# One routed-expert transformer block: where the first expert's third weight piece is split into two halves

## The chip, the core and the metric

The kernel runs on one core of a Trainium2 chip. The number that counts is the device time in microseconds (us) of one execution. TensorE (PE) multiplies matrices, VectorE (DVE), ScalarE (ACT) and GpSimd (POOL) compute element by element, and SyncE (SP) issues most of the DMAs. Each engine runs its own instructions in order; they meet through semaphores only.

## The reference

The block takes x (4 batches of 1024 tokens, 256 wide) and does two steps, each added to x:

```python
x = x + tanh(g_xattn) * xattn(layernorm(x), ctx, ctx, mask)      # 77 keys per batch
x = x + tanh(g_ffn) * ffn(layernorm(x))
# ffn: every token goes to the one expert (of 8) with the largest router probability
logits = x @ router_w + router_b
for e in range(8):
    a, g = split(x @ w1[e]); y = silu(a) * g @ w2[e]     # w1[e] 256 x 2048, w2[e] 1024 x 256
    out = where(argmax == e, y, out)
out = out * max_prob
```

## The kernel before

**Attention loop.** The 1024 positions are cut into 8 groups of 128, each for all 4 batches. A software pipeline of 10 iterations (`for i in range(NG + 2)`) exists on each engine: in iteration i, PE makes the scores of group i and attends for group i - 2, ACT copies transposed x out of PSUM and takes the exponentials, DVE adds the mask, finds the maximum, adds the attention to x (L810) and takes the statistics of the second layernorm (L819, L825), POOL turns these into a reciprocal root and the router's logits (`norm2`, L423 to L432).

**Weights as two halves.** The expert matmuls run in a format that keeps part of a float32's bits. Every weight w is therefore held as w_hi (the rounded value) and w_lo = w - w_hi, and the products with w_hi and w_lo are added up. An expert has three pieces of 2048 columns (`PIECES` = 3): the two halves of w1 along the contraction (`DC` = 2), then w2. A piece is loaded by SP into `staging`, copied by ACT into `w_hi`, and POOL writes `w_lo` = `staging` - `w_hi`. For the first expert this is done in six chunks of 1024 columns (`N_CHUNK` = 6, chunks 4 and 5 are the third piece): `high0(c)` on ACT (L597) at the end of iteration c, `low0(c)` on POOL (L439) at the end of iteration c + 1. After every second chunk POOL raises `w_ready`. All other experts' pieces are split inside the expert loop (L723 on ACT, L511 on POOL).

**Building the lists.** When the last logits are there, each engine leaves the loop. DVE takes the argmax, sums the exponentials that ACT made (L659), writes the gate (L869), and turns counts and ranks into the position of each token in a list sorted by expert (L876 to L892). It then builds, in three rounds, one-hot tables in float16 (L908, L910, L913) that PE multiplies (L1133) into the list of indices; between the rounds PE runs matmuls whose result nobody reads (L1138). POOL writes two index ramps (iota, L460 and L462) for these tables before. It waits then for the first list (`lists_ready`) and gathers the rows of the first 128 sorted tokens with an indirect DMA (L467). ACT has nothing to do until it copies the tables of tile numbers out of PSUM (L663).

**Expert loop.** 35 tiles of 128 sorted tokens. For each, PE does the products with w1 (`up`, L1161), transposes, and those with w2 (`down`, L1179). The first tile's `up` waits for `w_ready`; in the loop, `down` of the tile before waits for `w_ready` of its own expert's third piece, an existing wait (`old * PIECES + PIECES`). SP's load of the second expert's third piece into `staging` waits for `w_ready` at 3, and that of the first piece for 1.

Of the kernel before, what the change touches and what calls it, by code (L numbers as in the profile page):

```python
# [27 lines left out]
def flamingo_block(nc, x, ctx_kv, mask, g_xattn, g_ffn, w1, b1, w2, b2, router_w, router_b, e_w1, e_w2, out):  # L28
    B, S, D = x.shape
    KEYS = ctx_kv.shape[1]  # L30
    E, _, F2 = e_w1.shape
    F = F2 // 2
    DC = D // P
# [13 lines left out]
    PIECES = 3  # L47
    PW = F2
# [26 lines left out]
    with ExitStack() as top:  # L75
# [5 lines left out]
        def sem(name):  # L81
            return top.enter_context(nc.semaphore(name))
# [214 lines left out]
        w_ready = sem("w_ready")  # L297
# [18 lines left out]
        W_CHUNK = PW // 2  # L316
# [2 lines left out]
        QUARTERS = 4  # L319
        QW = PW // QUARTERS  # L320
        N_CHUNK = PIECES * PW // W_CHUNK

        block = top.enter_context(nc.Block())

# [41 lines left out]
        def _(pool):  # L366
# [28 lines left out]
            def norm1(first_group, end_group):  # L395
                n = (end_group - first_group) * B
                at = slice(first_group, end_group)
                if first_group == 1:
                    pool.wait_ge(square_ready, 1)
                    link(nc.gpsimd.tensor_scalar(var_eps1[:, 1], x_square[:], 1.0 / D, EPS, ALU.mult, ALU.add))  # L400
                else:
                    pool.wait_ge(mv1_ready, end_group if end_group == 1 else end_group - 1)
                    link(nc.gpsimd.tensor_scalar(var_eps1[:, at], mv1[:, at, :, 1], EPS, None, ALU.add))
                nc.gpsimd.tensor_tensor(out=rstd1[:, at], in0=var_eps1[:, at],
                                        in1=minus_half[:, 0:n].rearrange("p (g b) -> p g b", b=B),
                                        op=ALU.pow).then_inc(rstd1_ready, end_group - first_group)

            def mask1(g):
                if g == 0:
                    pool.wait_ge(mask_loaded, 16)  # L410
                    pool.wait_ge(bias_ready, 1)
                if g >= 2:
                    pool.wait_ge(masked_ready, g - 1)
                nc.gpsimd.tensor_tensor(out=mask_c[:, g % 2], in0=bias_c[:].rearrange("p (b k) -> p b k", b=B),
                                        in1=mask_in[:, g:g + 1, :].to_broadcast([P, B, KEYS]),
                                        op=ALU.add).then_inc(mask_c_ready, 1)

            def norm2(g):
                r = g % 2
                pool.wait_ge(mv2_ready, g + 1)  # L420
                if g >= SHARED:
                    pool.wait_ge(half2_ready, g - SHARED + 1)
                link(nc.gpsimd.tensor_scalar(var_eps2[:, r], mv2[:, r, :, 1], EPS, None, ALU.add))  # L423
                link(nc.gpsimd.tensor_tensor(out=x_all[:, g, :, 1], in0=var_eps2[:, r], in1=minus_half[:, 0:B], op=ALU.pow))  # L424
                link(nc.gpsimd.tensor_tensor(out=logit_tmp[:], in0=x_all[:, g, :, KEPT:XROW],
                                             in1=x_all[:, g, :, 1:2].to_broadcast([P, B, E]), op=ALU.mult))
                if g == 0:
                    pool.wait_ge(router_b_loaded, 16)
                nc.gpsimd.tensor_tensor(out=logits[:, g * B:(g + 1) * B], in0=logit_tmp[:],
                                        in1=router_b_all[:].unsqueeze(1).to_broadcast([P, B, E]),  # L430
                                        op=ALU.add).then_inc(logits_ready, 1)
                nc.gpsimd.tensor_tensor(out=x_all[:, g, :, 0], in0=mv2[:, r, :, 0], in1=x_all[:, g, :, 1],  # L432
                                        op=ALU.mult).then_inc(rstd2_ready, 1)

            def low0(c):

                pool.wait_ge(w_hi_ready, c + 1)
                at = slice(c * W_CHUNK, (c + 1) * W_CHUNK)
                lo = nc.gpsimd.tensor_tensor(out=w_lo[:, at], in0=staging[:, at], in1=w_hi[:, at].bitcast(FP32),  # L439
                                             op=ALU.subtract)  # L440
                if c % 2:
                    lo.then_inc(w_ready, 1)
# [7 lines left out]
            for i in range(NG + 2):  # L450
                if i + 2 < NG:
                    mask1(i + 2)
                if 0 <= i - 2 < NG:
                    norm2(i - 2)
                if i < NG - EARLY:
                    norm1(EARLY + i, EARLY + i + 1)
                if 0 <= i - 1 < N_CHUNK:
                    low0(i - 1)
            pool.wait_ge(first_stored, 16 * FIRST)
            nc.gpsimd.iota(slot_iota[:], [[1, P], [0, B]], base=0, channel_multiplier=0,  # L460
                           allow_small_or_imprecise_dtypes=True)
            nc.gpsimd.iota(col_iota[:], [[1, COLS], [0, B]], base=0, channel_multiplier=0,  # L462
                           allow_small_or_imprecise_dtypes=True).then_inc(iotas_ready, 1)


            def gather_rows(t, index):
# [36 lines left out]
            def low_part(t):  # L503

                piece = pool.value_load(tile_piece[:, bass.ds(t, 1)], min_val=0, max_val=E * PIECES - 1)
                with pool.If(piece > 0):
                    src = pool.snap((piece % PIECES) * PW)
                    dst = pool.snap(((piece // PIECES) & 1) * EW + src)
                    pool.wait_ge(w_hi_ready, piece + (N_CHUNK - PIECES + 1))
                    for q in range(QUARTERS):  # L510
# [28 lines left out]
        def _(act):  # L539
# [25 lines left out]
            def copy_xt(g):  # L565
                act.wait_ge(xt1_psum, g + 1)
                if g >= 2:
                    act.wait_ge(scores_psum, g - 1)
                for k in range(DC):
                    last = nc.scalar.copy(x_t[:, g % 2, k], ps_xt[k][:])  # L570
                last.then_inc(xt1_ready, 1)
# [20 lines left out]
            def high0(c):  # L592

                if c % 2 == 0:
                    act.wait_ge(piece_loaded, 16 * (c // 2 + 1))
                at = slice(c * W_CHUNK, (c + 1) * W_CHUNK)
                nc.scalar.copy(w_hi[:, at], staging[:, at]).then_inc(w_hi_ready, 1)  # L597

            def copy_pt(g):
                act.wait_ge(pt_psum, g + 1)  # L600
                if g >= 2:
                    act.wait_ge(attn_psum, B * (g - 1))
                nc.scalar.copy(probs_t[:, g % 2], ps_p[0:KEYS, :]).then_inc(pt_ready, 1)

            def copy_logits(g):
                act.wait_ge(masked_ready, g + 1)
                scored = ps_s[g % 2][:, 0:B * KW].rearrange("p (b k) -> p b k", b=B)
                nc.scalar.copy(x_all[:, g, :, KEPT:XROW], scored[:, :, KEYS:KW]).then_inc(x_logits_ready, 1)

            def softmax(g):  # L610
                r = g % 2
                act.wait_ge(max_ready, g + 1)
                if g >= 2:
                    act.wait_ge(pt_psum, g - 1)
                    act.wait_ge(inv_ready, g - 1)
                for b in range(B):
                    last = nc.scalar.activation(probs[:, r, b], masked[:, r, b], ACT.Exp, bias=neg_max[:, r, b:b + 1],
                                                accum_out=prob_sum[:, r, b:b + 1])
                last.then_inc(probs_ready, 1)

            for i in range(NG + 1):
                if i + 1 < NG:
                    copy_xt(i + 1)
                if 0 <= i - 1 < NG:
                    copy_pt(i - 1)
                if i < NG:
                    copy_logits(i)
                    softmax(i)
                if i < N_CHUNK:
                    high0(i)  # L630


# [23 lines left out]
            for part, (first_group, end_group) in enumerate(PARTS):  # L656
                at = slice(first_group * B, end_group * B)
                act.wait_ge(centered, part + 1)
                nc.scalar.activation(work_e[:, at], work_b[:, at], ACT.Exp).then_inc(gate_exp, 1)  # L659


            act.wait_ge(tab_psum, 1)
# [325 lines left out]
        def _(pe):  # L988
# [153 lines left out]
            def transpose_x(t):  # L1142

                pe.wait_ge(xnorm_ready, t + 1)
                for k in range(DC):
                    last = nc.tensor.transpose(px[:, k * P:(k + 1) * P], x_norm[:, k * P:(k + 1) * P], ident[:])  # L1146
                last.then_inc(xt_psum, 1)
# [36 lines left out]

            pe.sem_inc(down_psum[1], 1)
            transpose_x(0)
            pe.wait_ge(w_ready, PIECES)
            pe.wait_ge(lists_ready, 2)
            up(0, 0, 0)
            up(0, 1, 0)  # L1190
# [56 lines left out]
```

## Time and profile before

| what | us |
|---|---|
| median of 3 runs (lowest, highest) | 437.21 (436.66, 441.84) |
| the profiled execution, its own time | 438.43 |
| its span, first to last instruction | 436.4 |
| PE busy in it | 401.4 (92%) |
| DVE, ACT, POOL busy | 194.4, 212.2, 239.7 |

The span is what the trace covers; the execution's own time is 2.03 us longer. In the span, the attention loop and what is prepared for it end at about 68 us, the lists are built up to 84.1 us, and the expert tiles follow from 89.9 us. "Busy" counts computing instructions alone; what decides is which engine the others wait for in each stage.

### The profile page before, as it was taken

What the parts mean: (1) busy time and instruction counts of PE and PEld (TensorE: products, weight loads), DVE (VectorE), ACT (ScalarE), POOL (GpSimd) and SP (SyncE); (2) the same over time, 40 slices, a digit from 0 to 9 for tenths busy, and PEclk for the clock granted to TensorE, in tenths of its full rate; (3) what the DMA queues carried; (4) which work ended last, traced back from release to release, by engine and by line L of the source; (5) the groups of instructions that cost most, each with busy time, mean ns of one, the idle gap of its engine ahead of it and who ended that gap; (6) DMA issues with size and microseconds to landing.
All of it is one profiled execution on the core that took longest, in us unless ns stands there. A gap on an engine that the chain in (4) does not pass through costs nothing.

```text
span 436.4 us, 9945 instructions
## 1 busy us (share of the span) xinstructions
PE 401.4 (92%) x2460; PEld 349.5 (80%) x2461; DVE 194.4 (45%) x464; ACT 212.2 (49%) x456; POOL 239.7 (55%) x315
## 2 busy tenths in 40 slices
PE   7988981679999999999999999999999999999990
PEld 7887860458888888888888888888888888888880
DVE  2888998714334343333434333333343343334330
ACT  2785752047536556645633364455534563433330
POOL 2588885115774887778842267648732785322221
PEclk9998997689999999999999999999999999999996
DMA  7952225634540333444331014403340010010010
GB/s 204 355 176 98 97 99 147 107 112 128 206 135 24 120 120 118 177 149 151 120 120 30 30 63 172 132 19 120 120 132 24 21 31 24 24 36 16 24 36 12
DMA packets 29850, 44.01 MB, mean 101 GB/s; under 512 B 8377, under 2 KB 25581, under 8 KB 27791
## 3 DMA queue, kind: packets, MB, share of 16 engines
q1 hardware_dynamic: 24095, 34.45, 24.5%
q0 software_dynamic: 3456, 9.11, 6.5%
q10 hardware_dynamic: 2288, 0.33, 0.5%
q8 instruction: 4, 0.07, 0.1%
q14 instruction: 7, 0.06, 0.0%
HBM read 35.44 MB, written 8.83 MB: 101 GB/s over the span
## 4 chain that ended last, share of the span: by engine, by line
PE 78%; DVE 8%; DMA 4%; SPq 3%; issue 3%; ACT 1%; POOL 1%; POOLq 0%; DVEq 0%; ACTq 0%
PE pa L1161 22%; PE pg L1161 22%; PE py L1179 22%; PE ph L1171 7%; SPq L333 3%; DMA staging<-in_L_ffn_w 2%; DVE x_all L810 2%; PE px L1146 2%; DVE bn L819 1%; PE ps_s L1083 1%; DVE masked L791 1%; DMA x_sorted<-residual_rows,idx_gather 1%; PE ps_xt L997 1%; DMA out<-out_tile,idx_now 1%; POOL x_all L424 0%
## 5 line engine op out<-in xcount | busy, mean ns | idle before, releaser
L511 POOL TENSOR_TENSOR w_lo<-staging,w_hi x84 | 105.9, 1290 | 6.5 <-ACT w_hi L723 3.9
L954 DVE TENSOR_TENSOR ht_lo<-ph,ht_hi 128x512 fp32r<-128x512 f32 x70 | 48.4, 692 | 133.9 <-ACT ht_hi L700 133.9
L700 ACT CAST ht_hi<-ph 128x512 fp32r<-128x512 f32 x70 | 41.1, 588 | 119.2 <-PE ph L1171 85.8
L1179 PE MATMUL py<-w_hi,ht_hi 128*128 x272 | 78.9, 290 | 0.0
L1179 PE MATMUL py<-w_hi,ht_lo 128*128 x272 | 76.1, 280 | 0.0
L1179 PE MATMUL py<-w_lo,ht_hi 128*128 x272 | 76.0, 279 | 0.0
L500 POOL DMA_INDIRECT out<-out_tile,idx_now x34 | 34.7, 1021 | 73.5 <-DVE out_tile L962 73.2
L1161 PE MATMUL pa<-w_hi,xt_hi 128*128 (+1 forms) x140 | 58.5, 418 | 0.8 <-ACT xt_hi L672 0.8
L467 POOL DMA_INDIRECT x_sorted<-residual_rows,idx_now x34 | 35.7, 1049 | 38.4 <-ACT residual L688 20.8
L1161 PE MATMUL pg<-w_hi,xt_hi 128*128 (+1 forms) x140 | 55.9, 399 | 0.0
L1161 PE MATMUL pa<-w_lo,xt_hi 128*128 (+1 forms) x140 | 55.9, 399 | 0.0
L1161 PE MATMUL pa<-w_hi,xt_lo 128*128 (+1 forms) x140 | 55.8, 399 | 0.0
L1161 PE MATMUL pg<-w_hi,xt_lo 128*128 (+1 forms) x140 | 55.8, 398 | 0.0
L1161 PE MATMUL pg<-w_lo,xt_hi 128*128 (+1 forms) x140 | 55.3, 395 | 0.0
L949 DVE TENSOR_TENSOR hidden<-pg,silu 128x512 f32<-128x512 f32 x70 | 48.1, 687 | 8.1 <-ACT silu L694 4.9
L1179 PEld LDWEIGHTS py<-w_lo,ht_hi 128*128 128x128 f32 x272 | 51.2, 188 | 0.0
L1179 PEld LDWEIGHTS py<-w_hi,ht_hi 128*128 128x128 f32 x272 | 51.2, 188 | 0.0
L1179 PEld LDWEIGHTS py<-w_hi,ht_lo 128*128 128x128 f32 x272 | 51.1, 188 | 0.0
L723 ACT CAST w_hi<-staging x21 | 40.2, 1912 | 9.7 <-PE py L1179 7.8
L694 ACT ACTIVATE silu<-pa 128x512 f32<-128x512 f32 x70 | 42.3, 605 | 3.5 <-PE pg L1161 3.5
L1171 PE MATMUL ph<-ident,hidden 128*128 128x128 f32 x280 | 41.9, 272 | 0.0
L942 DVE TENSOR_TENSOR xt_lo<-px,xt_hi 128x256 fp32r<-128x256 f32 x36 | 15.3, 424 | 59.0 <-ACT xt_hi L672 59.0
(194 smaller groups left out, 630.1 us busy)
## 6 DMA issues: line engine op xcount, KB each, us to landing
staging<-in_L_ffn_w SPq DMA_DIRECT2D x24, 1024.0 KB
residual_rows<-x_all SPq DMA_DIRECT2D x8, 516.0 KB, 3.8
x_all<-in_x SPq DMA_DIRECT2D x8, 512.0 KB, 10.0
x_sorted<-residual_rows,idx_now POOLq DMA_INDIRECT x34
out<-out_tile,idx_now POOLq DMA_INDIRECT x34, 2.5
w_in<-in_L_xattn_W SPq DMA_DIRECT2D x2, 256.0 KB, 4.7
ctx_in<-in_ctx SPq DMA_DIRECT2D x1, 308.0 KB
mask_in<-in_fside_1xSxS ACTq DMA_DIRECT2D x1, 308.0 KB, 11.6
```

The source lines that it names most:

```text
L467: pool.indirect_dma_start(x_sorted[:], None, rows, bass.IndirectOffsetOnAxis(ap=index, axis=0), bounds_check=last_row(t), oob_is_err=False ...
L500: pool.indirect_dma_start(out_rows, bass.IndirectOffsetOnAxis(ap=idx_now[:, 1:2], axis=0), tile_rows[:], None, bounds_check=limit, oob_is_ ...
L511: lo = nc.gpsimd.tensor_tensor(out=w_lo[:, bass.ds(dst + q * QW, QW)], in0=staging[:, bass.ds(src + q * QW, QW)], in1=w_hi[:, bass.ds(dst ...
L694: nc.scalar.activation(silu[:, j], pa[j][:], ACT.Silu).then_inc(silu_ready[j], 1)
L700: nc.scalar.copy(ht_hi[:, j], ph[j][:]).then_inc(hhi_ready[j], 1)
L723: nc.scalar.copy(w_hi[:, bass.ds(slot + src, PW)], staging[:, bass.ds(src, PW)]).then_inc(w_hi_ready, 1)
L942: nc.vector.tensor_tensor(out=xt_lo[:], in0=px[:, 0:D].rearrange("p (k n) -> p k n", k=DC), in1=xt_hi[:].bitcast(FP32), op=ALU.subtract).t ...
L949: nc.vector.tensor_tensor(out=hidden[:, j], in0=pg[j][:], in1=silu[:, j], op=ALU.mult).then_inc(hidden_ready[j], 1)
L954: nc.vector.tensor_tensor(out=ht_lo[:, j], in0=ph[j][:], in1=ht_hi[:, j].bitcast(FP32), op=ALU.subtract).then_inc(hlo_ready[j], 1)
L1161: last = mm(ps[:], xt[:, k], w[:, bass.ds(slot + (k * PW + col), HALF)], start=n == 0, stop=n == 3 * DC - 1)
L1171: last = nc.tensor.transpose(ph[j][:, c * P:(c + 1) * P], hidden[:, j, c * P:(c + 1) * P], ident[:])
L1179: last = mm(into[:, 0:D], ht[:, j, c * P:(c + 1) * P], w[:, bass.ds(slot + (DC * PW + (j * HC + c) * D), D)], start=j == 0 and n == 0, sto ...
```

## The change

Chunks 4 and 5, the two halves of the third piece, leave the loop on ACT and POOL. ACT does `high0(4)` and `high0(5)` after its last exponential, POOL does `low0(4)` and `low0(5)` after its second iota. PE's first `up` now waits for two pieces instead of three. Chunks 0 to 3 stay where they are; no instruction is added or dropped.

```diff
+        LOOP_CHUNK = DC * PW // W_CHUNK
...
                 if i < NG - EARLY:
                     norm1(EARLY + i, EARLY + i + 1)
-                if 0 <= i - 1 < N_CHUNK:
+                if 0 <= i - 1 < LOOP_CHUNK:
                     low0(i - 1)
             pool.wait_ge(first_stored, 16 * FIRST)
             nc.gpsimd.iota(slot_iota[:], [[1, P], [0, B]], base=0, channel_multiplier=0,
                            allow_small_or_imprecise_dtypes=True)
             nc.gpsimd.iota(col_iota[:], [[1, COLS], [0, B]], base=0, channel_multiplier=0,
                            allow_small_or_imprecise_dtypes=True).then_inc(iotas_ready, 1)
+            for c in range(LOOP_CHUNK, N_CHUNK):
+                low0(c)
...
-                if i < N_CHUNK:
+                if i < LOOP_CHUNK:
                     high0(i)
...
                 nc.scalar.activation(work_e[:, at], work_b[:, at], ACT.Exp).then_inc(gate_exp, 1)
+            for c in range(LOOP_CHUNK, N_CHUNK):
+                high0(c)
...
-            pe.wait_ge(w_ready, PIECES)
+            pe.wait_ge(w_ready, DC)
```

POOL's order before, from the end of iteration 6 to the first gather; L439 is `low0(5)`, and `low0(4)` stands seven rows above it:

```order
L439 TENSOR_TENSOR w_lo<-staging,w_hi 128x1024
L423 TENSOR_SCALAR var_eps<-mv 128x4
...
L432 TENSOR_TENSOR x_all<-mv,x_all 128x4
L460 IOTA slot_iota 128x512
L462 IOTA col_iota 128x220
L467 DMA x_sorted<-residual_rows,idx_gather 128x259 x3
```

POOL's order in the changed kernel, for the same place (its lines count one more from here on):

```order
L424 TENSOR_SCALAR var_eps<-mv 128x4
...
L433 TENSOR_TENSOR x_all<-mv,x_all 128x4
L461 IOTA slot_iota 128x512
L463 IOTA col_iota 128x220
L440 TENSOR_TENSOR w_lo<-staging,w_hi 128x1024 x2
L470 DMA x_sorted<-residual_rows,idx_gather 128x259 x3
```

Both subtractions now stand between the iotas and the gather, behind the last `norm2`.

ACT's order before, iteration 5 of the loop and, after the dots, the place behind the loop (L597 is `high0`, L659 the exponentials for the gate, L663 the tables):

```order
L617 ACTIVATE probs,prob_sum<-masked,neg_max 128x77 x4
L597 CAST w_hi<-staging 128x1024
L570 COPY x_t<-ps_xt 128x512 x2
...
L659 ACTIVATE work_e<-work_b 128x224
L659 ACTIVATE work_e<-work_b 128x32
L663 CAST tables<-ps_p 4x128
```

and in the changed kernel:

```order
L620 ACTIVATE probs,prob_sum<-masked,neg_max 128x77 x4
L573 COPY x_t<-ps_xt 128x512 x2
...
L662 ACTIVATE work_e<-work_b 128x224
L662 ACTIVATE work_e<-work_b 128x32
L600 CAST w_hi<-staging 128x1024 x2
L668 CAST tables<-ps_p 4x128
```

The two copies stand behind the gate's exponentials and ahead of the tables' copy.

## Rows read from the trace of the kernel before

**Rows 1.** The page, part 4: shares of the chain that ended last

```profile
PE 78%; DVE 8%; DMA 4%; SPq 3%; issue 3%; ACT 1%; POOL 1%; POOLq 0%; DVEq 0%; ACTq 0%
```

**Rows 2.** Timeline, ACT, loop: start us, us, instruction, [idle before <- releaser]

```profile
47.66 1.07 ACT L570 COPY x_t<-ps_xt 128x512 f32<-128x512 f32 x2 [1.48 <-PE ps_xt L997]
...
50.56 1.04 ACT L597 CAST w_hi<-staging 128x1024 fp32r<-128x1024 f32 x1
52.73 1.07 ACT L570 COPY x_t<-ps_xt 128x512 f32<-128x512 f32 x2 [1.12 <-PE ps_xt L997]
```

**Rows 3.** Timeline, POOL, loop, around chunks 4 and 5

```profile
54.78 2.36 POOL L439 TENSOR_TENSOR w_lo<-staging,w_hi 128x1024 fp32r<-128x1024 f32 x1
57.60 0.23 POOL L423 TENSOR_SCALAR var_eps<-mv 128x4 f32<-128x4 f32 x1 [0.46 <-DVE mv L825]
...
62.95 0.23 POOL L423 TENSOR_SCALAR var_eps<-mv 128x4 f32<-128x4 f32 x1 [0.87 <-DVE mv L825]
```

**Rows 4.** Timeline, DVE: L810 beside a POOL subtraction (43.74), and without one (62.96)

```profile
43.74 1.79 DVE L810 SCALAR_TENSOR_TENSOR x_all<-ps_o,prob_inv,x_all 128x264 f32<-128x264 f32 x4 [1.53 <-PE ps_o L1092]
...
62.96 1.79 DVE L810 SCALAR_TENSOR_TENSOR x_all<-ps_o,prob_inv,x_all 128x264 f32<-128x264 f32 x4
```

**Rows 5.** Timeline, ACT and POOL, list building: what bounds the idle stretches

```profile
86.45 0.26 ACT L663 CAST tables<-ps_p 4x128 int32<-4x128 f32 x1 [14.66 <-PE ps_p L1140]
...
72.35 0.59 POOL L462 IOTA col_iota<- 128x220 f16 x1
84.77 1.30 POOL L467 DMA_INDIRECT x_sorted<-residual_rows,idx_gather  x1 [11.83 <-DVE idx_scatter L923]
```

**Rows 6.** Timeline, DVE, list building: five of its instructions

```profile
73.07 0.24 DVE L869 TENSOR_SCALAR gate<-recip,tanh_g 128x32 f32<-128x32 f32 x1
...
73.23 0.68 DVE L876 TENSOR_TENSOR_SCAN cum<-restart,ps_xt 128x256 f32<-128x256 f16 x1
...
73.95 0.17 DVE L878 TENSOR_SCALAR counts_i<-cum 128x8 int32<-128x8 f32 x1
...
74.57 0.17 DVE L881 TENSOR_TENSOR_SCAN bounds<-restart,tiles_f 128x8 f32<-128x8 f16 x1
...
75.30 0.42 DVE L885 TENSOR_TENSOR work_a<-work_a,shift 128x256 f32<-128x256 f32 x1
```

**Rows 7.** The chain in order of time: start us, us, what

```profile
73.31 0.61 DVE cum L876
...
93.67 0.43 PE pa L1161
...
99.43 0.23 PE pa L1161
```

**Rows 8.** Timeline, DVE and POOL, three pairs of overlapping instructions

```profile
11.15 0.29 DVE L761 COPY bq_wide<-bq 128x256 f32<-128x256 f32 x1
11.16 0.37 POOL L403 TENSOR_SCALAR var_eps<-mv 128x4 f32<-128x4 f32 x1 [7.92 <-DVE mv L743]
...
70.26 0.39 DVE L862 TENSOR_TENSOR onehot<-expert_m,first 128x224 f16<-128x224 f32 x1
70.37 0.38 POOL L425 TENSOR_TENSOR logit_tmp<-x_all 128x32 f32<-128x32 f32 x1
...
69.25 1.04 POOL L424 TENSOR_TENSOR x_all<-var_eps,minus_half 128x4 f32<-128x4 f32 x1
69.41 0.39 DVE L858 SCALAR_TENSOR_TENSOR work_a<-work_b,expert_m 128x224 f32<-128x224 f32 x1
```

**Rows 9.** Timeline, POOL: the two stretched forms elsewhere

```profile
18.25 0.23 POOL L403 TENSOR_SCALAR var_eps<-mv 128x4 f32<-128x4 f32 x1 [0.36 <-DVE mv L743]
...
64.39 0.24 POOL L425 TENSOR_TENSOR logit_tmp<-x_all 128x32 f32<-128x32 f32 x1
```

**Rows 10.** Windows: stretch, us, PE busy, PEld, DVE, ACT, POOL, PEclk, DMA share, GB/s

```profile
75.00:78.00 3.00, 0.00 (x0) 0.00 (x0) 2.79 (x9) 0.00 (x0) 0.00 (x0) 0.50 0.98 42
...
91.00:94.40 3.40, 3.40 (x10) 2.66 (x9) 0.00 (x0) 0.07 (x1) 0.02 (x1) 0.51 0.22 49
```

## The prediction

> **What bounds the kernel now.** I read the shares of the chain of waits first: PE holds 78% of it and DVE 8% [rows 1]. Those shares are an average over stages, so I then read the chain in order of time around the two places that the change touches. In the attention loop it runs through DVE almost without a break. From 73.31 us, while the lists are built, it runs through DVE again and through PE's list matmuls, up to POOL's first gather at 84.77; in the expert tiles it runs through PE [rows 5, 7]. So the first place, which loses work, and the second, which gets it, are both stages where DVE sets the pace. The question is whether ACT's and POOL's work costs DVE anything in either.
>
> **What leaves the loop.** On ACT, two copies of 1.04 us. Behind the later one ACT sits idle for 1.12 us until PE has transposed the next group [rows 2]; the earlier one is followed by 1.48 us of such idling. Work that is followed by a longer wait for somebody else wasn't on the path, so the gain is 0. On POOL, two subtractions of 2.36 us. Behind the first POOL waits 0.46 us for DVE's statistics, behind the second 0.87 us [rows 3]: gain 0 too. Nor do these subtractions slow DVE in the loop: L810, which has one operand in SBUF and one in PSUM, takes 1.79 us for four both beside a subtraction and without one [rows 4]. A gain above 0 would need a wait that the rows don't show. Its upper bound is what POOL gives up, 2 x 2.36 = 4.7 us, and the rows with idle behind them place it at 0. I take 0.
>
> **What is added behind the loop, on ACT.** The two copies, 2.1 us, go into an idle stretch of 14.66 us that ends at 86.45 and so begins at 71.79 [rows 5]. They would run from 71.7 to 73.8. What covers them is ACT's wait for the tables, and 12 us of it are left. Cost 0. DVE's sum of exponentials isn't delayed, since the copies stand behind them.
>
> **On POOL.** The iotas end at 72.94, the gather follows at 84.77 after 11.83 us of idling [rows 5]. Two subtractions of 2.36 us fit: `low0(4)` from 72.9 to 75.25 (its w_hi half is there at 72.75), `low0(5)` at the earliest from 75.2 to 77.6. The gather queued behind them isn't reached by that time, so directly they cost 0. The wait for `w_ready` 3 moves from PE's first `up` at 89.9 to its first `down`, later still, and at 77.6 it is long met. SP's loads that wait for `w_ready` 1 and 2 are fed by chunks that don't move, and the load that needs 3 stands in SP's queue behind the wait for the second gather, which comes after 84.77. All 0.
>
> **The indirect cost: DVE beside POOL.** This is the term that decides. In the new place the subtractions read SBUF without pause for 4.7 us, and DVE runs its chain of small dependent steps beside them. Unlike L810, many of these have all operands in SBUF: L869 and L878 are tensor-by-scalar operations with source and result there, L881 and L885 read two SBUF tensors each [rows 6]. Two pairs of the trace show that such DVE instructions and POOL's exclude each other. POOL's L403 takes 0.37 us when it starts 0.01 us behind DVE's 256-column copy, and ends 0.09 us after that copy; elsewhere it takes 0.23. POOL's L425 takes 0.38 us beside DVE's two-input L862, and ends 0.10 us after it; elsewhere 0.24 [rows 8, 9]. In both POOL came second and was held by 0.14 us until DVE was done. A third pair speaks against the reverse: POOL's L424 was running for 0.16 us when DVE's two-input L858 started, and L858 took its usual 0.39 [rows 8]. But L424 handles four elements in 1.04 us, so it hardly reads, while a subtraction of 1024 columns reads all the time; for that no DVE instruction of the exposed kinds overlaps anywhere in this trace. So the bounds are:
> - none held: 0.
> - only two-input instructions held, subtractions as whole units: L881, due at 74.57, goes at 75.25 (+0.7). `low0(5)` gets in behind it and runs to about 77.8. L885, due at 75.30 + 0.7, goes at 77.8: 77.8 - 75.3 = +2.5.
> - tensor-by-scalar held as well, DVE served between the two subtractions: L869, due at 73.07, goes at 75.2 (+2.1). `low0(5)` gets in behind it, 75.4 to 77.8. L876 reads PSUM and one SBUF tensor and passes [rows 6]. L878, due at 73.95, goes at 77.8: +3.9.
> - POOL keeps its turn for both: L869 goes at 77.6, 77.6 - 73.07 = +4.5.
>
> I take +3.9: the first of the exclusion pairs is a copy, a one-input instruction like the tensor-by-scalar ones, and in both pairs the loser waited for the whole instruction. A hold on DVE here isn't absorbed, because the chain has no gap from 73.31 to the gather [rows 7]: PE's list matmuls, `lists_ready`, the gather and the first `up` all come 3.9 us later. The ends 0 and 4.5 make the range. A DVE instruction that starts first holds POOL instead, but POOL has 7 us in hand.
>
> The Trainium skill, "SBUF — State Buffer", section "Who interferes with whom", says just this of the shared port pair: a DVE instruction with two SBUF inputs, against POOL instructions that read SBUF, or in a two-port mode (copy, cast, tensor_scalar), shuts out POOL or is shut out by it for the whole instruction, whoever issues first. By that rule the term is the third bound, and it speaks against this change. The trace agrees for the two pairs in which DVE came first (0.14 us each) and doesn't for the pair in which POOL did.
>
> **TensorE's clock.** It stands at 0.50 (1.2 GHz) from 75 to 78 us, with PE idle, and at 0.51 from 91.0 to 94.4, with PE busy throughout [rows 10]. In that last stretch some 8 matmuls follow one another at 0.43 instead of 0.23 us [rows 7], 8 x 0.2 = 1.6 us lost against 2.4 GHz. If the first tile starts later, this stretch could move, vanish or repeat. No row says which; I enter 0 with ends of -1.6 and +1.6.
>
> **The sum.** 0 - 0 + 0 + 3.9 = +3.9 us on the span of 436.4, so 440.3. The profiled execution took 438.43, 1.2 us above the median; the median of 437.21 lies 0.8 us above the span. I forecast for the median: 437.2 + 3.9 = **441.1 us**.
>
> **Rivals.**
> 1. *Nothing is held* (the other side: no slower). POOL's long subtraction lets DVE read in between, as L424 did with L858. Everything moved lies under DVE's chain: 437.2. It decides as soon as a hold lasts a few hundredths of a microsecond instead of the whole 2.36. For it: the third pair. Against it: the two stretched POOL instructions. Chance 0.22.
> 2. *The loop gets shorter*, by a coupling that the rows don't show, say half of POOL's smaller slack turned around, or the clock's dip at 91 vanishes: -0.5 to -1.6, so 435.6 to 436.7. For it, nothing but that the loop loses 6.8 us of ACT and POOL work. Chance 0.06.
> 3. *Held, and the clock's dip lasts longer or comes twice*: +3.9 + 1.6, so 442.7, up to 443.3 with +4.5. PE's idle stretch ahead of its list matmuls would grow by the 3.9 us, at a clock that is at 0.50 in it already [rows 10]. Against it: the matmuls that nobody reads (L1138) stand between list and first tile as before. Chance 0.12.
> 4. *The forecast*, pair held, with its smaller form of +2.5 (439.7): chance 0.60.
>
> **Range and chances.** The likeliest time is 441.1. The range is 436.3 to 443.3: its upper end is that of rival 3, its lower end takes in half of rival 2. In between lie the forecast in its forms, the no-hold case and most of rival 3; for the noise of runs some of each falls outside, which leaves about 0.8. About 2% (8.7 us) is what a measurement of this kernel can tell from no change, its runs having spread over 5 us. None of the cases reaches it: within 2% 0.95, slower 0.04 for a second loss on top of the hold, faster 0.01.
>
> **What would show each step.** In the changed profile: both subtractions at about 72.9 and 75.4; the gate's L869 lasting some 2.3 us instead of 0.24, or starting late, and the count step L878 some 1.8 instead of 0.17; the sum over the DVE instructions between 73 and 84 larger by 3.9, their number unchanged. The gather at about 88.7 instead of 84.77. The loop ending at the same time as before. From the first `up` to the end the same length, within 1.5. I would be wrong if every small DVE step kept its 0.17 beside the subtractions (rival 1), if the loop ended earlier (rival 2), or if the hold were real but ended with each of POOL's reads, giving some tenths in all.

## The result, and the profile after

Over 22 executions each, the changed kernel's median is 441.16 us (lowest 440.00, highest 446.92), that of the kernel before 438.38 (436.57 to 444.39). The ratio is 1.0059, 95% interval 1.0036 to 1.0083: slower by some 2.6 us (1.6 to 3.6 us), well inside 2%. The lowest executions differ by 3.43 us. The forecast was 441.1 us, and +3.9 against before, which lies above that interval. (Executions of either kernel lie between 436 and 448 us, with a mean granted clock of TensorE between 0.971 and 0.938, so the lowest ones are the cleanest to compare, and two medians only with their spread.)

The profiled execution of the changed kernel took 445.69 us: span 443.6, 7.2 above the profiled one of before. It must be taken apart before anything is read from it. First DVE's timeline in the list building (start us, us, instruction):

```profile
77.13 2.22 DVE L874 TENSOR_SCALAR gate<-recip,tanh_g 128x32 f32<-128x32 f32 x1
79.28 0.67 DVE L881 TENSOR_TENSOR_SCAN cum<-restart,ps_xt 128x256 f32<-128x256 f16 x1
...
79.98 1.65 DVE L883 TENSOR_SCALAR counts_i<-cum 128x8 int32<-128x8 f32 x1
81.67 0.17 DVE L884 TENSOR_SCALAR tiles_i<-counts_i 128x8 int32<-128x8 int32 x1
...
82.08 0.18 DVE L886 TENSOR_TENSOR_SCAN bounds<-restart,tiles_f 128x8 f32<-128x8 f16 x1
```

and POOL and ACT in the same place:

```profile
76.41 0.59 POOL L463 IOTA col_iota<- 128x220 f16 x1
76.97 4.64 POOL L440 TENSOR_TENSOR w_lo<-staging,w_hi 128x1024 fp32r<-128x1024 f32 x2
92.25 1.30 POOL L470 DMA_INDIRECT x_sorted<-residual_rows,idx_gather  x1 [10.65 <-DVE idx_scatter L928]
...
75.75 1.97 ACT L600 CAST w_hi<-staging 128x1024 fp32r<-128x1024 f32 x2
```

The gate's step, which took 0.24 us [rows 6], takes 2.22; the count step, 0.17 before, takes 1.65. That is 1.98 + 1.48 = 3.46 us. Nothing else in DVE's list building is longer: the tiles step behind them has its 0.17 again, and the two-input step L886, which the second bound of the prediction would have had held, comes when POOL is through, at 76.97 + 4.64 = 81.61.

The chain in order of time (start us, us, what) shows that both lie on the path:

```profile
77.13 2.22 DVE gate L874
79.35 0.61 DVE cum L881
...
79.98 1.66 DVE counts_i L883
...
97.35 0.76 PE pa L1166
```

The last row is the first product with w1. In the kernel before it stands at:

```profile
89.91 0.47 PE pa L1161
```

Where the rest of the 7.2 us is, the windows of the two kernels tell (stretch, us, PE busy, PEld, DVE, ACT, POOL, PEclk, DMA share, GB/s), before first:

```profile
63.00:73.00 10.00, 3.12 (x12) 1.83 (x12) 9.02 (x29) 5.03 (x20) 7.60 (x17) 0.87 0.38 134
```

```profile
63.00:73.00 10.00, 8.14 (x20) 5.88 (x20) 8.16 (x28) 5.10 (x19) 4.02 (x11) 0.50 0.35 121
```

In this execution TensorE ran at 0.50 (1.2 GHz) in the last part of the attention loop, and PE, busy for 8.14 instead of 3.12 us there, became what DVE waits for. That is only half of what the loop lost. The gate's step starts at 77.13 instead of 73.07, 4.06 later, and 2.13 of these us were already gone when DVE took its last full set of four statistics (L824, which is L819 of before), at 63.18 instead of 61.05. Up to there too the clock was lower than in the profile of before: 0.71 against 0.77 from 36 to 43 us, 0.93 against 1.00 from 43 to 63. The sum: 4.06 (up to the gate's step) + 3.46 (DVE held) = 7.52. The first product comes 7.44 later, and what follows takes 346.25 instead of 346.49. From the start of the gate's step to that product it is 20.22 us instead of 16.84, so 3.38 of the 3.46 arrives there. Only this part is the change's as far as the experiments show.

### The profile page after: what moved, and what is told of

It is laid out like the page before. It is cut to its first block, busy times and chain, and to the rows that moved or that the text cites. A ratio compares the mean times of both kernels' runs of the same rounds, so it can differ in the third digit from the quotient of the medians.

```text
span 443.6 us, 9945 instructions
## 1 busy us (share of the span) xinstructions
PE 405.6 (91%) x2460; PEld 352.9 (80%) x2461; DVE 198.3 (45%) x464; ACT 211.7 (48%) x456; POOL 239.5 (54%) x315
## 4 chain that ended last, share of the span: by engine, by line
PE 80%; DVE 8%; DMA 4%; SPq 3%; issue 2%; ACT 1%; POOL 1%; POOLq 0%; DVEq 0%; ACTq 0%
PE pa L1166 22%; PE pg L1166 22%; PE py L1184 22%; PE ph L1176 7%; SPq L334 3%; DMA staging<-in_L_ffn_w 2%; PE ps_o L1097 2%; DVE x_all L815 2%; PE px L1151 2%; PE ps_s L1088 1%; DVE bn L824 1%; DVE masked L796 1%; DMA x_sorted<-residual_rows,idx_gather 1%; PE ps_xt L1002 1%; DMA out<-out_tile,idx_now 1%
```

## The experiments

Each is compared with runs of the kernel before on the same chip. In the diffs, a line with + is new against the changed kernel.

**1. The changed kernel again.** No edit. Is the low clock in the loop part of the change?

> The changed kernel once more. Theory (DVE is held by POOL's subtractions): the gate's tensor-by-scalar step lasts about 2.2 us again instead of 0.24, the count step about 1.65 instead of 0.17, and the time is 3.5 us above the kernel before. That the clock stood at 1.2 GHz from 63 to 73 us in the first profile is a matter of the single execution, so that stretch is not there in most executions. Rival (the change itself costs clock in the attention loop): the stretch of 1.2 GHz comes again and the loop ends 4 us later again, 77.1 instead of 73.1 us for the start of the gate's step.

Measured: median 443.5 us (lowest 440.41), ratio 1.0118 (1.0062 to 1.0174). The profiled execution is the lowest one, with a span of 438.4:

```profile
73.20 2.22 DVE L874 TENSOR_SCALAR gate<-recip,tanh_g 128x32 f32<-128x32 f32 x1
...
76.06 1.65 DVE L883 TENSOR_SCALAR counts_i<-cum 128x8 int32<-128x8 f32 x1
```

The two long steps are the same to the hundredth, and the gate's step starts 0.13 us behind that of before. So the holds come with the change, and the 4 us ahead of them do not come in every execution of it. On the stretch at 1.2 GHz, theory and rival were each wrong in part. It is there again (a window, columns as above):

```profile
63.00:73.00 10.00, 4.82 (x12) 2.83 (x10) 8.00 (x27) 5.62 (x21) 6.70 (x16) 0.50 0.37 129
```

but the loop does not end 4 us later. This execution had the full clock from 36 to 43 us (1.00, against 0.77 before) and took those last four statistics at 59.98, 1.07 ahead of before. It then lost 1.20 up to the gate's step. So the clock ahead of 63 us counts too, and PEclk in one window doesn't tell when the loop ends.

The first product with w1 starts at 93.42, 3.51 later than before, yet the span is only 2.0 us longer. Behind that product lie 345.0 us against 346.5. The chain shows where: this execution kept the full clock at the first tile, its matmuls taking 0.23 us each, while in that of before those from 91.11 to 94.10 took 0.43 [rows 7], at a clock of 0.51 [rows 10]:

```profile
93.42 0.47 PE pa L1166
...
95.06 0.23 PE pa L1166
...
97.86 0.24 PE pa L1166
```

The two measurements of this same kernel, 1.0059 and 1.0118, have intervals that meet at 1.006 to 1.008; the spread of the executions is wider than the effect, and the profiles tell more than the medians.

**2. Only POOL's part.** ACT makes its copies in the loop as before.

```diff
-                if i < LOOP_CHUNK:
+                if i < N_CHUNK:
                     high0(i)
...
-            for c in range(LOOP_CHUNK, N_CHUNK):
-                high0(c)
```

> Only POOL's subtractions are moved; ACT makes its copies in the loop as before. Theory: the whole cost is there, +3.5 us, the gate's step at 2.2 and the count step at 1.65 us. Rival (ACT's copies are part of it): less than 2 us above the kernel before.

Measured: median 442.81 (lowest 440.56), ratio 1.0101 (1.0044 to 1.0158). The gate's step takes 2.22 and the count step 1.65 us:

```profile
73.41 2.22 DVE L872 TENSOR_SCALAR gate<-recip,tanh_g 128x32 f32<-128x32 f32 x1
...
76.26 1.65 DVE L881 TENSOR_SCALAR counts_i<-cum 128x8 int32<-128x8 f32 x1
```

Both holds come with POOL's subtractions; ACT's copies aren't needed for them.

**3. One chunk instead of two**, on both engines.

```diff
-        LOOP_CHUNK = DC * PW // W_CHUNK
+        LOOP_CHUNK = N_CHUNK - 1
```

> Only the last chunk is moved, on both engines. Theory (a hold lasts to the end of POOL's instruction and DVE is served in between): the gate's step is held to the end of the one subtraction, +2.0 us, and the count step lasts 0.17 us; the time is 2.0 us above the kernel before. Rival (DVE is slowed in proportion to POOL's work): +1.7 us, spread over several steps of DVE. Rival (POOL keeps its turn until its queue is empty): the same +2.0 here.

Measured: median 440.42 (lowest 437.49), ratio 1.0058 (1.002 to 1.0096).

```profile
73.45 2.22 DVE L874 TENSOR_SCALAR gate<-recip,tanh_g 128x32 f32<-128x32 f32 x1
...
76.30 0.17 DVE L883 TENSOR_SCALAR counts_i<-cum 128x8 int32<-128x8 f32 x1
```

One subtraction, one hold of 1.98 us, and the count step is free. The first product with w1 starts 2.3 us later than before, 0.38 of it because the gate's step starts at 73.45 instead of 73.07. A slowing in proportion is out: one step carries the whole of it.

**4. The subtractions behind the first two gathers.** The same work, a place where I believed DVE had nothing exposed to do.

```diff
-            for c in range(LOOP_CHUNK, N_CHUNK):
-                low0(c)
...
                 gather_rows(t, idx_gather[:, t:t + 1])
+                if t < 2:
+                    low0(LOOP_CHUNK + t)
```

> ACT's copies stay behind the loop, POOL's two subtractions go behind the issue of the first and of the second gather, where DVE has little to do. Theory: the DVE steps last 0.24 and 0.17 us again and the time is that of the kernel before, within 0.5 us. Rival (ACT's copies or the emptier loop cost the time): 3.5 us above the kernel before, as the change.

Measured: median 443.46 (lowest 440.16), ratio 1.012 (1.0075 to 1.0165): as slow as the change, which is what the rival had said. The profile says that it isn't the rival's reason. The gate and the count take 0.24 and 0.17 us, but DVE builds the table of tile numbers beside the first gather (DVE, then POOL):

```profile
84.92 3.30 DVE L938 SCALAR_TENSOR_TENSOR tab_k<-tab_k 128x1 f32<-128x1 f32 x1
88.25 0.15 DVE L940 TENSOR_SCALAR tab<-tab_k 128x1 f32<-128x1 f32 x1
```

```profile
84.50 1.30 POOL L468 DMA_INDIRECT x_sorted<-residual_rows,idx_gather  x1 [11.86 <-DVE idx_scatter L928]
85.83 2.36 POOL L440 TENSOR_TENSOR w_lo<-staging,w_hi 128x1024 fp32r<-128x1024 f32 x1
```

In the kernel before, the same step is L933:

```profile
85.19 0.16 DVE L933 SCALAR_TENSOR_TENSOR tab_k<-tab_k 128x1 f32<-128x1 f32 x1
```

L938 writes one element per partition and takes 3.30 us: it ends when the subtraction does, 85.83 + 2.36 = 88.19. PE's transpose of the tables, ACT's copy and everything that ACT does for the first tile wait for it, and the first product starts at 91.91, 2.0 us late. My expectation had missed the table. Against the profiled execution of before (438.43) this one, at 440.16, is 1.7 longer, which fits the late start. Between the lowest executions lie 3.7 us; the 1.7 beyond the late start would be the clock's low stretch at the first tile, which stands in both profiles (PEclk 0.83 from 92 to 100 us here, 0.85 before) and need not be in the lowest execution of before. That part isn't shown.

**5. The subtractions behind the second gather**, where the table is done.

```diff
-            for c in range(LOOP_CHUNK, N_CHUNK):
-                low0(c)
...
                 gather_rows(t, idx_gather[:, t:t + 1])
+                if t == 1:
+                    for c in range(LOOP_CHUNK, N_CHUNK):
+                        low0(c)
```

> ACT's copies stay behind the loop; both of POOL's subtractions go behind the issue of the second gather, where DVE has no step with all operands in SBUF left to do before the third gather. Theory (only the meeting of POOL's subtractions with such DVE steps costs time): every DVE step of the list building has its length of before, the first product with w1 starts at 89.9 us, and the time is that of the kernel before within 0.5 us in the lowest run. Rival (ACT's copies or the emptier loop cost something): 2 us or more above it in the lowest run.

Measured: ratio 1.0006 (0.9967 to 1.0045), lowest 436.54 against 436.31 for the kernel before in the same runs, median 439.91 against 438.37. The profiled execution, 443.62 us, has the low clock in the loop, as the changed kernel's first one, and that without any hold:

```profile
63.00:73.00 10.00, 7.72 (x20) 5.53 (x18) 8.16 (x28) 5.10 (x19) 4.36 (x12) 0.50 0.36 122
```

Its steps in the list building have the lengths of before, and the subtractions run beside the first expert tile:

```profile
76.72 0.24 DVE L875 TENSOR_SCALAR gate<-recip,tanh_g 128x32 f32<-128x32 f32 x1
...
77.60 0.17 DVE L884 TENSOR_SCALAR counts_i<-cum 128x8 int32<-128x8 f32 x1
```

```profile
94.02 1.00 POOL L468 DMA_INDIRECT x_sorted<-residual_rows,idx_gather  x1 [4.30 <-ACT residual L694]
95.04 4.70 POOL L440 TENSOR_TENSOR w_lo<-staging,w_hi 128x1024 fp32r<-128x1024 f32 x2
```

The first product comes at 94.16 here, not at the 89.9 expected, and no hold is in that: 3.65 us lie ahead of the gate's step, and 0.6 behind the lists, where the tables wait for PE's unread matmuls at a low clock (0.64 from 88 to 90 us).

The executions of the two kernels match when they are sorted by their mean granted clock: at 0.964 they take 439.84 to 440.00 us against 439.83 to 439.96 before, at 0.951 441.47 and 441.86 against 441.71 to 441.98, and the profiled one, 443.62 at 0.945, has its like in one of before, 443.75 at 0.945. So the two copies on ACT, the emptier loop and PE's weaker wait show no cost and no gain, within the interval of the ratio, and POOL's subtractions cost by what they meet.

**6. Meeting the one-hot tables instead.** Are DVE steps with two inputs in SBUF held as well?

```diff
+            pool.wait_ge(pos_ready, 1)
             for c in range(LOOP_CHUNK, N_CHUNK):
                 low0(c)
```

> As the changed kernel, but POOL waits for the positions before its two subtractions, so that they meet the one-hot tables (two float16 inputs in SBUF, written one element after another) in place of the gate and the count. Theory (two-input steps are held too, to the end of POOL's instruction): one or two of the one-hot steps last 2 us longer, together 2.3 to 4.6 us, and the time is up by as much. Rival (only tensor-by-scalar steps are held): every one-hot step keeps its 0.50 or 0.95 us, POOL's subtractions keep their 2.36, and the time is that of the kernel before.

Measured: median 442.72 (lowest 439.65), ratio 1.0068 (1.0029 to 1.0108).

```profile
77.50 0.50 DVE L914 TENSOR_TENSOR col_hot<-col_iota,pos_f 128x660 f16<-128x660 f16 x1
77.92 3.10 DVE L916 TENSOR_TENSOR slot_hot<-slot_iota,pos_f 128x1536 f16<-128x1536 f16 x1
80.94 2.63 DVE L919 TENSOR_TENSOR col_hot<-col_hot,token_v 128x660 f16<-128x660 f16 x1
83.49 0.49 DVE L914 TENSOR_TENSOR col_hot<-col_iota,pos_f 128x660 f16<-128x660 f16 x1
```

```profile
77.55 5.66 POOL L440 TENSOR_TENSOR w_lo<-staging,w_hi 128x1024 fp32r<-128x1024 f32 x2 [4.48 <-DVE pos_f L898]
```

In the kernel before, the two steps that are longer here are:

```profile
77.79 0.95 DVE L910 TENSOR_TENSOR slot_hot<-slot_iota,pos_f 128x1536 f16<-128x1536 f16 x1
78.66 0.49 DVE L913 TENSOR_TENSOR col_hot<-col_hot,token_v 128x660 f16<-128x660 f16 x1
```

They are longer by 3.10 - 0.95 = 2.15 and 2.63 - 0.49 = 2.14: 4.3 us. POOL pays too: its two take 5.66 instead of 4.64 us, for DVE came first in L914 and got in between the two. The hold is mutual, and each of these lasted until the other engine's instruction was done.

**7. Quarters.** Each subtraction in four of 256 columns.

```diff
-                low0(c)
+                pool.wait_ge(w_hi_ready, c + 1)
+                for q in range(4):
+                    at = slice(c * W_CHUNK + q * 256, c * W_CHUNK + (q + 1) * 256)
+                    lo = nc.gpsimd.tensor_tensor(out=w_lo[:, at], in0=staging[:, at], in1=w_hi[:, at].bitcast(FP32),
+                                                 op=ALU.subtract)
...
```

> As the changed kernel, with each subtraction cut into four of 256 columns, some 0.7 us each. Theory (a hold ends with POOL's present instruction, and DVE and POOL then take turns): the gate's step is held for 0.7 us at most, and so is every exposed step behind it, up to 0.7 each, until POOL is through: together 3.5 to 4.8 us. Rival (POOL keeps its turn as long as its next instruction is ready): the gate's step alone is held, for all 5.6 us. Rival (holds shrink with the instruction and don't repeat): less than 1.5 us in all.

Measured: median 440.96 (lowest 439.24), ratio 1.0051 (1.0011 to 1.0091).

```profile
77.28 0.60 DVE L880 TENSOR_SCALAR gate<-recip,tanh_g 128x32 f32<-128x32 f32 x1
...
78.52 0.72 DVE L889 TENSOR_SCALAR counts_i<-cum 128x8 int32<-128x8 f32 x1
79.27 0.65 DVE L890 TENSOR_SCALAR tiles_i<-counts_i 128x8 int32<-128x8 int32 x1
79.95 0.65 DVE L891 TENSOR_SCALAR tiles_f<-tiles_i 128x8 f32<-128x8 int32 x1
80.63 0.65 DVE L892 TENSOR_TENSOR_SCAN bounds<-restart,tiles_f 128x8 f32<-128x8 f16 x1
81.32 0.64 DVE L894 TENSOR_SCALAR shift<-bounds 128x8 f32<-128x8 f32 x1
```

The two engines take turns. Each hold is shorter, but there are seven: 0.36 + 0.55 + 0.48 + 0.48 + 0.48 + 0.47 and 0.16 in the next two-input step with both in SBUF (L896), 3.0 us together, against 3.5 to 4.8 expected and 3.46 for the whole chunks. Both rivals are out: the gate's step isn't held for all of POOL's work, and the holds do repeat. Cutting POOL's work finer moves the cost about more than it removes it.

**8. Writes only.** The subtractions of the third piece are left out; two ramps to the staging buffer and zeros to w_lo stand in their place.

```diff
-                low0(c)
+                pool.wait_ge(w_hi_ready, c + 1)
+                at = slice(c * W_CHUNK, (c + 1) * W_CHUNK)
+                nc.gpsimd.iota(staging[:, at], [[1, W_CHUNK]], base=0, channel_multiplier=0, ...)
+            nc.gpsimd.memset(w_lo[:, LOOP_CHUNK * W_CHUNK:N_CHUNK * W_CHUNK].bitcast(FP32), 0.0).then_inc(w_ready, 1)
```

> As the changed kernel, but POOL's two subtractions of the first expert's third piece are left out; in their place POOL writes two ramps of 1024 numbers (some 2.4 us each) to the staging buffer and zeros to w_lo, all of which read nothing from SBUF. Theory (reading and writing are granted apart, and the tensor-by-scalar steps of DVE use both): the gate's step and the count step are held as in the changed kernel, 3.4 us in all. Rival (only POOL's reads shut DVE out): 0, the steps last 0.24 and 0.17 us.

Measured: median 441.3 (lowest 438.90), ratio 1.0034 (0.9992 to 1.0076). The ramps turned out shorter than I had put them, 0.97 us each, 3.7 us of writes in all:

```profile
75.72 0.85 DVE L878 TENSOR_SCALAR gate<-recip,tanh_g 128x32 f32<-128x32 f32 x1
75.88 0.69 DVE L885 TENSOR_TENSOR_SCAN cum<-restart,ps_xt 128x256 f32<-128x256 f16 x1
...
76.63 2.62 DVE L887 TENSOR_SCALAR counts_i<-cum 128x8 int32<-128x8 f32 x1
```

```profile
75.54 1.94 POOL L468 IOTA staging<- 128x1024 f32 x2
77.43 1.80 POOL L470 MEMSET w_lo<- 128x2048 f32 x1
```

Tensor-by-scalar steps are held by POOL's writes alone: the count step by 2.45 us. The gate's step is longer by 0.61, but the scan behind it starts 0.16 us after it, as before, so that one costs nothing. My theory (held, 3.4) is nearer than its rival (0), but it missed the size; 2.5 us are lost. The ratio alone would not show it, since its interval takes in 1.

**9. Writes only, meeting the one-hot tables**: the wait of experiment 6 ahead of the edit of experiment 8. There is one execution only, 437.44 us, whose time tells nothing beside a single one of before at 441.86; the rows are what counts.

> As the kernel that waits for the positions, with the subtractions of the first expert's third piece left out and the ramps and zeros of the write-only kernel in their place, so that POOL's writes alone meet the one-hot steps (two float16 inputs in SBUF). Theory (a two-input step uses only the shared way to read): every one-hot step keeps its 0.50 or 0.95 us. Rival (any POOL instruction shuts out any DVE step with all operands in SBUF): one or two of them last 0.9 to 1.8 us longer.

```profile
76.22 0.50 DVE L918 TENSOR_TENSOR col_hot<-col_iota,pos_f 128x660 f16<-128x660 f16 x1
76.64 0.95 DVE L920 TENSOR_TENSOR slot_hot<-slot_iota,pos_f 128x1536 f16<-128x1536 f16 x1
77.50 0.50 DVE L923 TENSOR_TENSOR col_hot<-col_hot,token_v 128x660 f16<-128x660 f16 x1
```

```profile
76.25 1.94 POOL L469 IOTA staging<- 128x1024 f32 x2 [4.47 <-DVE pos_f L902]
78.13 1.81 POOL L471 MEMSET w_lo<- 128x2048 f32 x1
```

Nothing is held, on either side. Two-input steps exclude POOL's reads (experiment 6), not its writes.

## Why the prediction was right, point by point

- **What leaves the loop: 0.** Right as far as the runs can tell. Experiment 5 has the same loop and the steps of before; its ratio of 1.0006 (0.9967 to 1.0045) shows no gain, and makes one of more than 1.5 us unlikely. One reading was too simple: the chain in the loop isn't almost all DVE's. In the profile of before it runs through PE from 37.73 to 43.65 us and through POOL's `norm2` from 62.95 to 65.1. In the first of these stretches the clock stood at 0.77 (36 to 43 us), so it bears on the loop's length, which the prediction didn't price.
- **ACT's copies: 0.** Right: experiment 2 leaves them in the loop and has the same two holds, experiment 5 moves them and has none.
- **POOL beside DVE: +3.9, third bound.** The mechanism is shown; the size was 3.46. The gate's step was put at +2.1 and measured +1.98. The count step was put at +1.8 and measured +1.48, and that is the mis-sized term: I let the second subtraction begin 0.2 us late, behind the gate's step, while POOL's two took 4.64 us together, the second starting within the last hundredths of the held step. I also let a held step begin where POOL's instruction ends, but it ended there: the gate's step at 77.13 + 2.22 = 79.35, the first subtraction at 76.97 + 2.35 = 79.32. The second bound (two-input steps only, +2.5) is out as the cause here, since L878 was held; that two-input steps are exposed as well is shown by experiment 6. The fourth bound, +4.5, is out: with one subtraction the gate's hold is the same 1.98.
- **The pair that spoke against a hold** (L858 beside the four-element L424 [rows 8]) wasn't a case of it, as I had argued by the size of the instruction. Whether it is the few elements that make the difference, no run here tells.
- **The rule of the Trainium skill**, "SBUF — State Buffer", section "Who interferes with whom". The trace agrees on which instructions exclude each other: two-input steps against POOL's reads (2.15 and 2.14 us in experiment 6) but not its writes (0 in experiment 9), and a `tensor_scalar` step, one of the kinds that can run in a two-port mode, against writes too (2.45 us in experiment 8); in which mode it ran, no profile shows. It says that whoever issues first has the pair. That held between gate and subtractions. It didn't in experiment 8, where the count step had waited since 76.63 and POOL's zeros, started at 77.43, went first; nor as far as the profile shows in experiment 4, below. (The profile has the start of an instruction, not its issue.)
- **The clock.** I entered 0 with ends of 1.6 to either side. The changed kernel has executions of both kinds: in its first profile the low stretch at the first tile is there, in the second it isn't, which gives back 1.5 us. That may be part of why the ratio of 1.0059 is 2.6 us and not 3.46; how often each kind comes, the profiles can't say, since they are single executions. I hadn't foreseen the loss in the loop, 4.06 us in the first profile. It comes to the version without any hold too (3.65 in experiment 5), and an execution of before has that version's time and mean clock (443.75 at 0.945, against 443.62). That speaks against its being the change's. Where the clock fell in that execution isn't known, since only one of before was profiled, and why it falls stays open.
- **The time**: 441.1 forecast, 441.16 measured. That is nearer than the working deserves, and it is luck. The median of before rose by 1.2 us with more executions, to 438.38, and the term was 0.4 too large. With both put right the sum is 438.38 + 3.46 = 441.84, 0.7 above what was measured; this rest is within the spread and has no shown cause.

## What to carry to other kernels

An engine that the profile shows idle is not free: ask what its neighbour is doing then. POOL's long elementwise instructions belong beside DVE work that reads PSUM (L810 [rows 4]), or reduces (before's L796 took its usual 0.47 us at 29.49, beside the subtraction that ran from 28.64 to 31.00), and not beside a chain of small dependent DVE steps with everything in SBUF, where one step of 0.17 us can cost the rest of POOL's instruction. Where POOL's work must overlap such steps, cutting it finer doesn't help much: one long meeting and many short ones cost about the same (3.46 and 3.0 us). Most holds ended with the POOL instruction then running, but not all: the table step of experiment 4 was held for 3.14 us by a queued subtraction of 2.36, and the count step of experiment 8 for 2.45 by two instructions in turn.

## What the runs showed that I had not expected

- In experiment 4 DVE's L938 was due at 84.92 and held until 88.2, although POOL was then still issuing its gather (84.50 to 85.80) and began the subtraction at 85.83. Beside the same gather without a subtraction behind it, the small steps weren't held (beside the changed kernel's gather at 92.25, L935 took 0.20 us and L938 itself 0.16). A queued POOL instruction seems to claim its way to SBUF ahead of its own start; that is an inference from this one case, and no other explanation was tested.
- Who is served first when POOL has the next instruction ready isn't uniform. DVE got in between two subtractions (the changed kernel, experiments 6 and 7), and did not between the ramp and the zeros (experiment 8). What decides it stays open.
- No version here beats the kernel before. Since the loop showed no gain from the emptier POOL and ACT, the best place found for the third piece (experiment 5) only equals the old one.
